# Halving the columns of some TensorE matmuls in a windowed-attention kernel, so that two steps are 1152 instructions

## The chip, the cores and the metric

The kernel runs on one core of a Trainium2 chip. The metric is the device time in microseconds (us) of one execution. The profiler's record of one execution stands beside it. TensorE is the matrix engine (PE in the profile, PEld its weight loads), DVE is VectorE, ACT is ScalarE, POOL is GpSimd, SP issues the transfers.

## The reference, cut to what matters

Input is `x` (16 sequences, 256 tokens, 128 channels), all fp32. A first part adds attention over windows of 64 tokens to it. The second part, on a layer norm of the result, runs six layers:

```python
for i in range(DEPTH):                                   # DEPTH = 6
    x = attn_layer(shift_tokens(x), Wqkv[i], q_scale[i], k_scale[i], Wo[i]) + x
    x = ffn_layer(shift_tokens(x), ln_g[i], ln_b[i], W1[i], b1[i], W2[i], b2[i]) + x

def attn_layer(x, Wqkv, qs, ksc, Wo):                    # 16 heads of 64, windows of 32
    q, k, v = heads(x @ Wqkv)                            # 128 -> 3 * 1024
    q, k = rotary(l2norm(q) * qs), rotary(l2norm(k) * ksc)
    sim = q @ k_of_own_and_previous_window * 8, masked
    return (softmax(sim) @ v).merge_heads() @ Wo         # 1024 -> 128
```

`ffn_layer` is a layer norm, a gated GELU layer of 2 x 341 columns and a product back to 128 channels.

## The kernel before, in words

The first part is a pipeline of its own over 32 tiles of 128 tokens (`first_stage`); it takes the first 280 us or so. The six layers then run as one pipeline whose unit is a block of 128 tokens: 32 blocks in a layer, 192 in all. The order of the work is written out by hand: each engine has a function (`step_pe`, `step_act`, `step_dve`, `step_pool`, `step_sp`) that is called for each step t = 0, 1, 2, ... and in it works on several blocks at once, block t in the projections, block t - 1 in the transposes and scores, block t - 3 in the weighted values and the output product. Everything is unrolled, so TensorE's program is one long stream of instructions without a branch in it. Engines meet by semaphores only.

Two steps make a pair, since a sequence has two blocks (`b = t % BLOCKS`, 0 or 1); in a step with b = 0 the feed-forward part does one share, in a step with b = 1 the other. On TensorE a step issues, in this order (before.py's lines 658 to 833):

1. `project` for q: six matmuls into one pair of banks. Each half of 512 columns (`UNIT`) has three, since a product of high and low parts takes the place of an fp32 one: high x high, low x high, high x low. The tokens (`xs_h`, `xs_l`) are the weights that are loaded, 128 x 128; 512 columns of `wq_h` or `wq_l` stream past. The type is F32R and such a matmul is one weight load and one matmul.
2. Eight transposes of the probabilities (`small,Sx`).
3. `project` for k, six matmuls.
4. Eight transposes of q (`small,qk`).
5. The weighted values, below called **the PT burst** (`PT,VB` and `PT,VA`): 64 fp32 matmuls with 64 x 64 weights and 32 columns. An fp32 matmul that is no transpose is issued as two weight loads and two matmuls, so the burst is 256 instructions, all in a row.
6. `project` for v, then eight transposes of k.
7. The share of the feed-forward part: with b = 0 the first product (`f_h,w_h`, `f_h,w_l`, `f_l,w_h`: 18 F32R matmuls of 256 columns), with b = 1 the second (`X,w_sb`), and four transposes.
8. The scores (`X,qT`): 32 fp32 matmuls with weights of 64 columns and 64 columns streaming.
9. The output product (`X,wo_sb`): eight fp32 matmuls, `PC[:, 0:P] += wo_sb[:, a, :].T @ oT[:, a, :]`, 128 x 128 weights and 128 columns streaming: 16 weight loads and 16 matmuls in the profile.

Who waits for this work: ACT squares q and k as soon as they are there (`q_done`, `k_done`), copies v (`v_done`), and DVE adds the output product to x (`y_done`, in `update_x`). Semaphore waits that don't fit on a matmul are instructions of their own in the stream. A helper records every matmul, so all have line 226 in the profile, and transposes 229; they are told apart by their tiles.

Of the kernel before, what the change touches and what calls it, by code (L numbers as in the profile page):

```python
# [13 lines left out]
P = 128  # L14
SEQS, LEN, DM = 16, 256, 128
TOKENS = SEQS * LEN
BLOCKS = LEN // P
# [5 lines left out]
INNER = HEADS * DH  # L23
PAIRS = HEADS // 2
UNIT = 512
KEYS = 2 * WIN
RING = 4
NBLOCKS = SEQS * BLOCKS
# [39 lines left out]
def build(nc, x_in, w_first, wqkv, wo, qkscale, fw1, fw2, vectors, c_rot, c_small, out):  # L68
    ctx = ExitStack()
    with ctx:  # L70
# [3 lines left out]
        def sem(name):  # L74
# [18 lines left out]
        wo_sb = sb("wo_sb", [P, PAIRS, DM])  # L93
# [23 lines left out]
        oT = flat_x1[:, KT:KT + INNER].rearrange("p (a q) -> p a q", a=PAIRS)  # L117
# [17 lines left out]
        PA0, PA1, PB, PC = (ctx.enter_context(nc.psum_tensor(f"pair{i}", [P, 1024], F32)) for i in range(4))  # L135
# [23 lines left out]
        S = {n: sem(n) for n in (*STEP, *PER_SEQ, *LOADS, *PARTS, *ONCE, *FIRST, "xf0", "xf1", "vb0", "vb1", "vb2", "vb3", "phase",   # L159
                                 "stored", "opened", "o_t", "o_sum", "zeroed",  # L160
                                 "cleared", "waited")}

        def apart(e):


            e.sem_inc(S["waited"], 1)
# [58 lines left out]
        def mm(out, lhsT, rhs, start=True, stop=True, **k):  # L225
            return T_.matmul(out, lhsT, rhs, start=start, stop=stop, **k)  # L226
# [385 lines left out]
        def blocks(pl, name, back, k):  # L612

            per = STEP[name]
            return pl.times(NBLOCKS * per) + ((pl.t - back) * per + k)
# [22 lines left out]
                for t in range(DRAIN, DRAIN + NBLOCKS):  # L638
                    step(e, pl.at(t))

        def project(layer, pair, high, low, first):
            w_high, w_low = wq_high[layer % 2], wq_low[layer % 2]
            for u in range(2):
                cols = slice(first + u * UNIT, first + (u + 1) * UNIT)
                out = pair[:, u * UNIT:(u + 1) * UNIT]
                mm(out, high, w_high[:, cols], True, False)
                mm(out, low, w_high[:, cols], False, False)
                last = mm(out, high, w_low[:, cols], False, True)
            return last

        def projections(t):
# [9 lines left out]
        def step_pe(e, pl):  # L661
            t, b, then = pl.t, pl.t % BLOCKS, (pl.t - 1) % 2
            one, other = projections(t)
            bank0, bank1, bank2 = feed_banks(t)
            fresh = t % NBLOCKS == 0
            layer = pl.turn + t // NBLOCKS
            if pl.has(0):
                if b == 0:
                    e.wait_ge(S["xs_ready"], seqs(pl, "xs_ready", t // BLOCKS, 2))
                s = (t // BLOCKS) % 2  # L670
                high, low = (x[:, s, b * P:(b + 1) * P] for x in (xs_h, xs_l))
                if pl.has(1):
                    e.wait_ge(S["rotated"], blocks(pl, "rotated", 1, 2))
                if pl.seq(11) is not None:
                    e.wait_ge(S["gated"], seqs(pl, "gated", pl.seq(11), 2))
                if pl.seq(12) is not None:
                    e.wait_ge(S["x_done"], seqs(pl, "x_done", SEQS + pl.seq(12), 1))
                if pl.seq(10) is not None:
                    e.wait_ge(S["x_kept"], seqs(pl, "x_kept", pl.seq(10), 1))
                if pl.last and pl.seq(14) is not None:  # L680
                    e.wait_ge(S["o_sum"], pl.seq(14) + 1)
                if fresh:
                    e.wait_ge(S["wq_low_q"], layers(pl, 2, t // NBLOCKS, 2))
                project(layer, one, high, low, 0).then_inc(S["q_done"], 1)
            if pl.has(3):
                e.wait_ge(S["weighed"], blocks(pl, "weighed", 3, 1))
                if pl.has(4):
# [5 lines left out]
                for a in range(PAIRS):  # L693
                    last = tr(PC[:, a * P:(a + 1) * P], Sx[:, then, a, :, :].rearrange("p w k -> p (w k)"))
                last.then_inc(S["pT_done"], 1)
            if pl.has(0):
                if pl.has(1):
                    e.wait_ge(S["v_kept"], blocks(pl, "v_kept", 1, 1))
                if fresh:
                    e.wait_ge(S["wq_low_k"], layers(pl, 2, t // NBLOCKS, 2))  # L700
                project(layer, other, high, low, INNER).then_inc(S["k_done"], 1)
            if pl.has(1):
                e.wait_ge(S["scaled"], blocks(pl, "scaled", 1, 1))
                if pl.has(3):
# [23 lines left out]
            if pl.has(0):  # L728
                e.wait_ge(S["rotated"], blocks(pl, "rotated", 0, 1))
                if fresh:  # L730
                    e.wait_ge(S["wq_low_v"], layers(pl, 2, t // NBLOCKS, 2))
                project(layer, one, high, low, 2 * INNER).then_inc(S["v_done"], 1)
            if pl.has(1):
                e.wait_ge(S["scaled"], blocks(pl, "scaled", 1, 2))
                e.wait_ge(S["qkT_kept"], blocks(pl, "qkT_kept", 1, 1))
# [49 lines left out]
            q = pl.seq(9)  # L785
            if q is not None:
                e.wait_ge(S["xn_done"], seqs(pl, "xn_done", q, 1))
                if pl.has(0):
                    e.wait_ge(S["rotated"], blocks(pl, "rotated", 0, 2))
                elif q:  # L790
                    e.wait_ge(S["x_kept"], seqs(pl, "x_kept", q - 1, 1))
                for h in range(BLOCKS):
                    last = tr(bank1[:, h * P:(h + 1) * P], f_xn[:, h, :])
                last.then_inc(S["turned_back"], 1)
# [27 lines left out]
                last.then_inc(S["s_done"], 1)  # L822
            if pl.has(3):
                e.wait_ge(S["o_kept"], blocks(pl, "o_kept", 3, 1))
                if pl.has(1):
                    e.wait_ge(S["qkT_kept"], blocks(pl, "qkT_kept", 1, 2))
                else:
                    e.wait_ge(S["pT_kept"], blocks(pl, "pT_kept", 3, 1))
                if (t - 3) % NBLOCKS == 0:
                    e.wait_ge(S["wo_loaded"], layers(pl, 16, (t - 3) // NBLOCKS, 16))  # L830
                for a in range(PAIRS):
                    last = mm(PC[:, 0:P], wo_sb[:, a, :], oT[:, a, :], a == 0, a == PAIRS - 1)
                last.then_inc(S["y_done"], 1)

        def step_act(e, pl):
# [397 lines left out]
        @block.sync  # L1233
        def _(sp):
            tiles_in = x_in.rearrange("(t p) d -> p t d", p=P)
            sp.dma_start(X1[:, 0:8, :], tiles_in[:, 0:8, :]).then_inc(S["x_in0"], 16)
            sp.dma_start(w1_raw[:, 0:w_first.shape[1]], w_first).then_inc(S["w_loaded"], 16)
            sp.dma_start(small[:, :], c_small).then_inc(S["c_loaded"], 16)
            sp.dma_start(X1[:, 8:16, :], tiles_in[:, 8:16, :]).then_inc(S["x_in1"], 16)
            sp.dma_start(X1[:, 16:24, :], tiles_in[:, 16:24, :]).then_inc(S["x_in2"], 16)  # L1240
            sp.dma_start(X1[:, 24:32, :], tiles_in[:, 24:32, :]).then_inc(S["x_in3"], 16)
            sp.dma_start(rot[:, :, :, :].rearrange("p a b c -> p (a b c)"), c_rot).then_inc(S["rot_loaded"], 16)
            sp.dma_start(wq_raw[:, :], wqkv[0, :, 0:INNER]).then_inc(S["wq_loaded"], 16)
            sp.dma_start(qks[:, :, :].rearrange("p a b -> p (a b)"), qkscale[0, :, :]).then_inc(S["qks_loaded"], 16)
            sp.dma_start(wo_sb[:, :, :].rearrange("p a b -> p (a b)"), wo[0, :, :]).then_inc(S["wo_loaded"], 16)
            sp.dma_start(w2_sb[:, :, :].rearrange("p a b -> p (a b)"), fw2[0, :, :]).then_inc(S["w2_loaded"], 16)
            sp.dma_start(vec_g[:, :], vectors[0, :, 0:2]).then_inc(S["g_loaded"], 16)
            sp.dma_start(vec_b1[:, :], vectors[0, :, 2:8]).then_inc(S["b1_loaded"], 16)
            sp.dma_start(vec_b2[:, :], vectors[0, :, 8:10]).then_inc(S["b2_loaded"], 16)
            for k in range(1, 3):  # L1250
                sp.wait_ge(S["wq_low_" + "qk"[k - 1]], 2)
                sp.dma_start(wq_raw[:, :], wqkv[0, :, k * INNER:(k + 1) * INNER]).then_inc(S["wq_loaded"], 16)
            for g in range(4):
                sp.wait_ge(S["a_resid"], nth("a_resid", 8 * g + 7))
                sp.dma_start(x1_kept[:, g * 8 * DM:(g + 1) * 8 * DM], flat_x1[:, g * 8 * DM:(g + 1) * 8 * DM]).then_inc(S["x1_stored"], 16)
            sp.wait_ge(S["cleared"], 1)
            sp.dma_start(w1_raw[:, :], fw1[0, :, :]).then_inc(S["fw1_loaded"], 16)
            steps(sp, step_sp)
            o = out.rearrange("(t p) d -> p t d", p=P)
            for q in range(SEQS):  # L1260
                sp.wait_ge(S["o_sum"], q + 1)
                sp.dma_start(o[:, q * BLOCKS:(q + 1) * BLOCKS, :], out_rows(q)).then_inc(S["stored"], 16)
            sp.wait_ge(S["stored"], 16 * SEQS)
# [36 lines left out]

        @block.tensor
        def _(pe):
            pe.wait_ge(S["c_loaded"], 16)
            pe.wait_ge(S["w_centred"], 1)
            first_stage(pe, first_pe)
            meet(pe, 1)
            pe.wait_ge(S["cleared"], 1)
            steps(pe, step_pe)
# [41 lines left out]
```

## Time and profile before

| | |
|---|---|
| time, median of 3 runs | 3254.94 us (3250.23 to 3259.81) |
| the profiled execution | 3258.42 us, of which the span of its instructions is 3256.6 us |
| mean granted clock of TensorE | 0.988 of full speed |
| TensorE matmul | 3119.6 us busy, 96% of the span |
| TensorE weight loads | 2720.0 us, 84% |
| VectorE | 2771.0 us, 85% |
| ScalarE | 2547.2 us, 78% |
| GpSimd | 2646.1 us, 81% |

The span and the execution's own time differ by 1.8 us, which lie around the first and the last instruction. Matmuls are pipelined, each recorded length overlaps the next; the time between the starts of two says what one costs in a row.

### The profile page before, as it was taken

What the parts mean: (1) busy time and instruction counts of PE and PEld (TensorE: products, weight loads), DVE (VectorE), ACT (ScalarE), POOL (GpSimd) and SP (SyncE); (2) the same over time, 40 slices, a digit from 0 to 9 for tenths busy, and PEclk for the clock granted to TensorE, in tenths of its full rate; (3) what the DMA queues carried; (4) which work ended last, traced back from release to release, by engine and by line L of the source; (5) the groups of instructions that cost most, each with busy time, mean ns of one, the idle gap of its engine ahead of it and who ended that gap; (6) DMA issues with size and microseconds to landing.
All of it is one profiled execution on the core that took longest, in us unless ns stands there. A gap on an engine that the chain in (4) does not pass through costs nothing.

```text
span 3256.6 us, 123131 instructions
## 1 busy us (share of the span) xinstructions
PE 3119.6 (96%) x52802; PEld 2720.0 (84%) x52802; DVE 2771.0 (85%) x3721; ACT 2547.2 (78%) x3699; POOL 2646.1 (81%) x2641
## 2 busy tenths in 40 slices
PE   7978999999999999999999999999999999999997
PEld 4646888888888888888888888888888888888886
DVE  7968888888888888888888888888888888888884
ACT  5756778887878788788878787887878787877876
POOL 6658888887888888888888888888888888888873
PEclk9989999999999999999999999999999999999999
DMA  2001111111111111111111111111111111111111
GB/s 66 15 19 38 46 40 43 41 39 43 37 46 48 40 36 46 37 48 41 46 36 41 37 53 41 41 39 42 39 46 46 43 35 41 41 44 39 40 39 49
DMA packets 62044, 134.01 MB, mean 41 GB/s; under 512 B 11584, under 2 KB 35264, under 8 KB 61504
## 3 DMA queue, kind: packets, MB, share of 16 engines
q1 hardware_dynamic: 61504, 126.14, 13.4%
q8 instruction: 421, 6.90, 0.9%
q14 instruction: 119, 0.97, 0.1%
HBM read 21.27 MB, written 4.19 MB: 8 GB/s over the span
## 4 chain that ended last, share of the span: by engine, by line
PE 91%; issue 3%; ACT 2%; POOL 2%; DVE 1%; DMA 0%; POOLq 0%; DVEq 0%; SPq 0%; ACTq 0%
PE pair L226 73%; PE pair L229 17%; POOL sq L414 1%; ACT qT L865 0%; ACT PT L846 0%; ACT sq L843 0%; POOL wq_l L977 0%; ACT X L882 0%; ACT X L870 0%; DVE VB L336 0%; ACT sq L855 0%; DVE qk L332 0%; ACT VA L878 0%; ACT qk L441 0%; DVE ts L993 0%
## 5 line engine op out<-in xcount | busy, mean ns | idle before, releaser
L1123 POOL TENSOR_TENSOR qk<-qk,ts 128x1024 f32<-128x1024 f32 x384 | 910.8, 2384 | 80.4 <-DVE ts L993 71.7
L1104 POOL TENSOR_TENSOR qk<-qk,rn 128x1024 f32<-128x1024 f32 x384 | 724.1, 1907 | 15.1
L989 DVE TENSOR_TENSOR qk<-pair,tab 128x1024 f32<-128x1024 f32 x384 | 468.5, 1220 | 271.5 <-ACT sq L843 265.8
L843 ACT ACTIVATE sq<-pair 128x1024 f32<-128x1024 f32 x192 | 196.9, 1025 | 445.2 <-PE pair L226 445.2
L226 PE MATMUL pair<-wq_h,xs_h 128*128 128x512 f32 x1154 | 513.8, 445 | 14.2 <-POOL xs_l L957 7.9
L1138 POOL TENSOR_TENSOR Sx<-Sx,rden 128x1024 f32<-128x1024 f32 x192 | 365.3, 1902 | 170.9 <-DVE rden L1055 170.9
L993 DVE TENSOR_TENSOR ts<-pair,tab 128x1024 f32<-128x1024 f32 x384 | 466.5, 1215 | 0.0
L997 DVE TENSOR_REDUCE ss<-sq 128x16 f32<-128x1024 f32 x384 | 464.2, 1209 | 0.0
L226 PE MATMUL pair<-wq_h,xs_l 128*128 128x512 f32 x1152 | 463.4, 402 | 0.7 <-issue 0.6
L226 PE MATMUL pair<-wq_l,xs_h 128*128 128x512 f32 x1152 | 462.1, 401 | 0.5 <-issue 0.3
L229 PEld LDWEIGHTS pair<-small,qk 128*128 128x128 f32 x3072 | 351.0, 143 | 84.7 <-issue 51.4
L229 PE MATMUL pair<-small,qk 128*128 128x128 f32 x3072 | 410.3, 277 | 6.9 <-POOL qk L1104 5.1
L226 PE MATMUL pair<-X,qT 128*64 128x64 f32 x12288 | 400.5, 224 | 8.5 <-ACT X L882 5.3
L226 PEld LDWEIGHTS pair<-X,qT 128*64 128x64 f32 x12288 | 374.0, 138 | 41.2 <-issue 41.2
L226 PE MATMUL pair<-PT,VA 64*64 64x32 f32 x12288 | 379.5, 219 | 25.6 <-issue 25.6
L226 PE MATMUL pair<-PT,VB 64*64 64x32 f32 x12288 | 380.7, 221 | 18.5 <-issue 16.1
L865 ACT ACTIVATE qT<-pair 64x1024 f32<-64x1024 f32 x384 | 389.7, 1015 | 6.4 <-PE pair L229 4.1
L226 PE MATMUL pair<-X,wo_sb 128*128 128x128 f32 x3072 | 393.9, 282 | 0.0
L226 PEld LDWEIGHTS pair<-PT,VB 64*64 64x64 f32 x12288 | 330.2, 135 | 55.6 <-issue 55.6
L226 PEld LDWEIGHTS pair<-X,wo_sb 128*128 128x128 f32 x3072 | 357.4, 192 | 12.9
L226 PEld LDWEIGHTS pair<-PT,VA 64*64 64x64 f32 x12288 | 332.6, 135 | 23.8 <-issue 23.8
L1010 DVE COPY pair<-small 128x1024 f32<-128x1024 f32 x192 | 235.7, 1228 | 61.6 <-ACT X L870 58.8
(124 smaller groups left out, 6672.2 us busy)
## 6 DMA issues: line engine op xcount, KB each, us to landing
VB<-VA SPq DMA_DIRECT2D x192, 384.0 KB, 3.5
VB<-VA SPq DMA_DIRECT2D x96, 128.0 KB, 3.5
wq_raw<-wqkv SPq DMA_DIRECT2D x18, 512.0 KB, 5.6
xf<-xT SPq DMA_DIRECT2D x96, 64.0 KB, 1.9
xf<-xT SPq DMA_DIRECT2D x96, 63.8 KB, 2.0
wo_sb<-wo SPq DMA_DIRECT2D x6, 512.0 KB, 3.5
X<-x_in SPq DMA_DIRECT2D x4, 512.0 KB, 6.7
x_kept<-X SPq DMA_DIRECT2D x4, 512.0 KB, 2.7
```

Source lines behind the costliest of these rows:

```text
L226: return T_.matmul(out, lhsT, rhs, start=start, stop=stop, **k)
L229: return T_.transpose(out, in_, ident if idn is None else idn)
L414: last = G_.tensor_tensor(h3(kx1[:, i % 2, w * UNIT:(w + 1) * UNIT], W1N), rep(kT1[:, w * W1N:(w + 1) * W1N], HALF1, W1N), bc(own_head, HA ...
L843: A_.activation(sq[:, 0, :], one[:, :], ACT.Square).then_inc(S["squared"], 1)
L865: last = A_.activation(qT[rows, :, :, odd * WIN:(odd + 1) * WIN], PC[rows, :].rearrange("p (a w q) -> p a w q", a=PAIRS, w=4), ACT.Copy)
L989: V_.tensor_tensor(h3(qk[:, now, kind, :], DH), h3(source[:, :], DH), rep(factors[:, 2 * kind, b, :], HEADS, DH), ALU.mult)
L993: V_.tensor_tensor(ts[:, kind, :].rearrange("p (h a c) -> p h a c", **halves), swapped, sines, ALU.mult).then_inc(S["rotated"], 1)
L997: V_.tensor_reduce(ss[:, kind * HEADS:(kind + 1) * HEADS], h3(sq[:, kind, :], DH), axis=AX.X, op=ALU.add).then_inc(S["summed"], 1)
L1010: V_.tensor_copy(h3(PB[:, :], P), rep(mask[:, bb * P:(bb + 1) * P], PAIRS, P)).then_inc(S["masked"], 1)
L1104: G_.tensor_tensor(x, x, bc(rn[:, then, kind * HEADS:(kind + 1) * HEADS], HEADS, DH), ALU.mult).then_inc(S["scaled"], 1)
L1123: G_.tensor_tensor(qk[:, now, kind, :], qk[:, now, kind, :], ts[:, kind, :], ALU.add).then_inc(S["added"], 1)
L1138: G_.tensor_tensor(x, x, bc(rden[:, now, :], HEADS, KEYS), ALU.mult).then_inc(S["weighed"], 1)
```

## The change

Four things, all of them on TensorE.

- `project` gets a number `halved`, 0 to 6: the last `halved` of its six matmuls are made in two halves of 256 columns. Per step with b = 0 these are 0 for q, 0 for k, 6 for v; with b = 1 they are 6, 6 and 5. With a few exceptions at layer changes and in the last layer, a pair of steps has 23 halved projection matmuls, that is 46 more instructions.
- The output product of a step with b = 0 is made in two halves of 64 columns for all eight of its matmuls (`WO_HALVED = (8, 0)`): 32 more instructions. The weights of a matmul are loaded again for its second half.
- Two waits that repeat an earlier one of the same engine are left out.
- 37 semaphore increments (`apart`) stand at the beginning of TensorE's stream, ahead of its first wait.

```diff
+        AHEAD = 37
+        HALVED = {0: (0, 0, 6), 1: (6, 6, 5)}
+        def halved(pl, k):
+            t, n = pl.t, HALVED[pl.t % BLOCKS][k]
+            if k == 2 and t == NBLOCKS:
+                n -= 1
+            if k == 2 and pl.last and pl.seq(13) is not None:
+                n -= 2 + t // BLOCKS % 2
+            return n
+        WO_HALVED = (8, 0)
-        def project(layer, pair, high, low, first):
+        def project(layer, halved, pair, high, low, first):
             w_high, w_low = wq_high[layer % 2], wq_low[layer % 2]
+            n = 0
             for u in range(2):
-                cols = slice(first + u * UNIT, first + (u + 1) * UNIT)
-                out = pair[:, u * UNIT:(u + 1) * UNIT]
-                mm(out, high, w_high[:, cols], True, False)
-                mm(out, low, w_high[:, cols], False, False)
-                last = mm(out, high, w_low[:, cols], False, True)
+                for x, w in ((high, w_high), (low, w_high), (high, w_low)):
+                    width = UNIT // 2 if n >= 6 - halved else UNIT
+                    for at in range(0, UNIT, width):
+                        last = mm(pair[:, u * UNIT + at:u * UNIT + at + width], x,
+                                  w[:, first + u * UNIT + at:first + u * UNIT + at + width],
+                                  n % 3 == 0 and at == 0, n % 3 == 2, skip_group_check=True)
+                    n += 1
             return last
...
-                if pl.has(0):
+                if pl.has(0) and pl.seq(11) is None:
                     e.wait_ge(S["rotated"], blocks(pl, "rotated", 0, 2))
...
-                if pl.has(1):
-                    e.wait_ge(S["qkT_kept"], blocks(pl, "qkT_kept", 1, 2))
-                else:
+                if not pl.has(1):
                     e.wait_ge(S["pT_kept"], blocks(pl, "pT_kept", 3, 1))
...
                 for a in range(PAIRS):
-                    last = mm(PC[:, 0:P], wo_sb[:, a, :], oT[:, a, :], a == 0, a == PAIRS - 1)
+                    width = P // 2 if a >= PAIRS - WO_HALVED[b] else P
+                    for at in range(0, P, width):
+                        last = mm(PC[:, at:at + width], wo_sb[:, a, :], oT[:, a, at:at + width], a == 0 and at == 0, a == PAIRS - 1,
+                                  skip_group_check=True)
...
         def _(pe):
+            for _ in range(AHEAD):
+                apart(pe)
             pe.wait_ge(S["c_loaded"], 16)
```

What this does to TensorE's stream, at two places. The first is the end of a step with b = 0 and the q projection of the step after it, before:

```order
L226 MATMUL pair<-X,qT 64x64 [waits masked,qkT_kept]
L226 MATMUL pair<-X,qT 64x64 x31
L226 MATMUL pair<-X,wo_sb 128x128 [waits qkT_kept,o_kept]
L226 MATMUL pair<-X,wo_sb 128x128 x7
L226 MATMUL pair<-wq_h,xs_h 128x512 [waits gated,rotated]
L226 MATMUL pair<-wq_h,xs_l 128x512
```

and after the change (the sizes are those of the output; an fp32 row of x1 is two weight loads and two matmuls):

```order
L226 MATMUL pair<-X,qT 64x64 [waits masked,qkT_kept]
L226 MATMUL pair<-X,qT 64x64 x31
L226 MATMUL pair<-X,wo_sb 128x64 [waits o_kept]
L226 MATMUL pair<-X,wo_sb 128x64 x15
L226 MATMUL pair<-wq_h,xs_h 128x256 [waits gated,rotated]
L226 MATMUL pair<-wq_h,xs_h 128x256
L226 MATMUL pair<-wq_h,xs_l 128x256 x2
```

Eight output products have become sixteen of half the width, with no work moved past another. The second place is what follows the PT burst of a step with b = 1, the v projection. Before:

```order
L226 MATMUL pair<-PT,VA 64x32 x4
L226 MATMUL pair<-wq_h,xs_h 128x512 [waits rotated]
L226 MATMUL pair<-wq_h,xs_l 128x512
L226 MATMUL pair<-wq_l,xs_h 128x512
L226 MATMUL pair<-wq_h,xs_h 128x512
```

and after the change:

```order
L226 MATMUL pair<-PT,VA 64x32 x4
L226 MATMUL pair<-wq_h,xs_h 128x512 [waits rotated]
L226 MATMUL pair<-wq_h,xs_l 128x256 x2
L226 MATMUL pair<-wq_l,xs_h 128x256 x2
L226 MATMUL pair<-wq_h,xs_h 128x256 x2
```

Five of the six matmuls are halved there. The order of the work is the same on every engine; only TensorE's stream has more instructions (115,109 where there were 107,919, counted as weight loads, matmuls and instructions that only wait or count), and a pair of steps has 1152 of them where it had 1077.

## Rows read from the trace of the kernel before

**Rows 1.** The page: span, busy time of each engine, and the chain that ended last

```profile
span 3256.6 us, 123131 instructions
...
PE 3119.6 (96%) x52802; PEld 2720.0 (84%) x52802; DVE 2771.0 (85%) x3721; ACT 2547.2 (78%) x3699; POOL 2646.1 (81%) x2641
...
PE 91%; issue 3%; ACT 2%; POOL 2%; DVE 1%; DMA 0%; POOLq 0%; DVEq 0%; SPq 0%; ACTq 0%
```

**Rows 2.** Stretches: length, busy time of PE, PEld, DVE, ACT, POOL, granted clock, DMA share, GB/s

```profile
893.20:924.40 31.20, 30.31 (x532) 26.91 (x531) 26.94 (x35) 24.77 (x35) 25.44 (x24) 1.00 0.22 66
924.40:958.80 34.40, 32.08 (x533) 28.29 (x532) 27.35 (x35) 24.86 (x35) 26.30 (x26) 0.95 0.12 33
1018.90:1049.10 30.20, 30.20 (x532) 26.78 (x531) 26.74 (x35) 24.68 (x35) 26.27 (x26) 1.00 0.13 37
...
928.10:931.50 3.40, 3.40 (x10) 2.71 (x11) 2.30 (x3) 1.54 (x2) 2.69 (x2) 0.50 0.02 5
```

**Rows 3.** What the matmuls that read PT waited for (the tile's view)

```profile
  issue: 41.7, 41
```

**Rows 4.** TensorE's timeline: end of a stalled PT burst; start and follower of an undisturbed one

```profile
942.39 0.32 PE L226 MATMUL pair<-PT,VB 64*64 64x32 f32 x8
...
943.70 0.30 PE L226 MATMUL pair<-PT,VA 64*64 64x32 f32 x8
944.97 0.26 PE L226 MATMUL pair<-PT,VB 64*64 64x32 f32 x5 [0.97 <-issue]
...
1003.55 0.32 PE L226 MATMUL pair<-PT,VB 64*64 64x32 f32 x8
...
1005.55 0.50 PE L226 MATMUL pair<-wq_h,xs_h 128*128 128x512 f32 x1
```

**Rows 5.** DMA queues of the page: packets, MB, share

```profile
q8 instruction: 421, 6.90, 0.9%
```

**Rows 6.** TensorE's timeline: matmuls of 512 and of 256 columns in a row

```profile
940.22 0.40 PE L226 MATMUL pair<-wq_h,xs_l 128*128 128x512 f32 x1
...
941.15 0.40 PE L226 MATMUL pair<-wq_l,xs_h 128*128 128x512 f32 x1
...
948.06 0.28 PE L226 MATMUL pair<-f_h,w_l 128*128 128x256 f32 x1
...
948.89 0.29 PE L226 MATMUL pair<-f_l,w_h 128*128 128x256 f32 x1
```

**Rows 7.** TensorE's timeline: whole runs of scores, output product, first stage

```profile
1010.34 2.09 PE L226 MATMUL pair<-X,qT 128*64 128x64 f32 x64
...
1012.36 2.05 PE L226 MATMUL pair<-X,wo_sb 128*128 128x128 f32 x16
1014.16 0.48 PE L226 MATMUL pair<-wq_h,xs_h 128*128 128x512 f32 x1
...
101.19 1.11 PE L226 MATMUL pair<-VA,PT 128*64 128x18 f32 x32
```

**Rows 8.** TensorE's timeline: the first matmuls of those runs and of one with 85 weight columns

```profile
1010.34 0.28 PE L226 MATMUL pair<-X,qT 128*64 128x64 f32 x2
1012.36 0.38 PE L226 MATMUL pair<-X,wo_sb 128*128 128x128 f32 x1
1009.47 0.35 PE L226 MATMUL pair<-f_h,w_h 128*85 128x256 f32 x1
```

**Rows 9.** Groups by form: weight loads, then matmuls (busy us, mean ns)

```profile
L226 PEld LDWEIGHTS pair<-X,qT 128*64 128x64 f32 x12288 | 374.0, 138 | 41.2 <-issue 41.2
L226 PEld LDWEIGHTS pair<-X,wo_sb 128*128 128x128 f32 x3072 | 357.4, 192 | 12.9
...
L226 PE MATMUL pair<-X,qT 128*64 128x64 f32 x12288 | 400.5, 224 | 8.5 <-ACT X L882 5.3 <-DVE pair L1010 3.2
L226 PE MATMUL pair<-X,wo_sb 128*128 128x128 f32 x3072 | 393.9, 282 | 0.0
L226 PE MATMUL pair<-VA,PT 128*64 128x18 f32 x1024 | 36.4, 214 | 0.0
```

More of the change, by code:

```diff
@@ L683, in step_pe @@
                     e.wait_ge(S["wq_low_q"], layers(pl, 2, t // NBLOCKS, 2))
-                project(layer, one, high, low, 0).then_inc(S["q_done"], 1)
+                project(layer, halved(pl, 0), one, high, low, 0).then_inc(S["q_done"], 1)
             if pl.has(3):
@@ L700, in step_pe @@
                     e.wait_ge(S["wq_low_k"], layers(pl, 2, t // NBLOCKS, 2))
-                project(layer, other, high, low, INNER).then_inc(S["k_done"], 1)
+                project(layer, halved(pl, 1), other, high, low, INNER).then_inc(S["k_done"], 1)
             if pl.has(1):
@@ L731, in step_pe @@
                     e.wait_ge(S["wq_low_v"], layers(pl, 2, t // NBLOCKS, 2))
-                project(layer, one, high, low, 2 * INNER).then_inc(S["v_done"], 1)
+                project(layer, halved(pl, 2), one, high, low, 2 * INNER).then_inc(S["v_done"], 1)
             if pl.has(1):
@@ L787, in step_pe @@
                 e.wait_ge(S["xn_done"], seqs(pl, "xn_done", q, 1))
-                if pl.has(0):
+                if pl.has(0) and pl.seq(11) is None:
                     e.wait_ge(S["rotated"], blocks(pl, "rotated", 0, 2))
-                elif q:
+                if not pl.has(0) and q:
                     e.wait_ge(S["x_kept"], seqs(pl, "x_kept", q - 1, 1))
```

## The prediction

> **What bounds the kernel now.** I begin with the page. TensorE is busy 96% of the span, and the chain that ended last runs through it for 91%, with 3% of "issue", time in which the engine waited for nothing that the profile shows [rows 1]. No other engine is over 85%. So TensorE's own stream sets the time, and a microsecond added to it should lengthen the kernel by one, as long as no other engine is near.
>
> The table of stretches shows that none is. I cut the six layers at the starts of the PT bursts, so that each stretch is one pair of steps. An undisturbed pair lasts 30.2 us and TensorE is busy for all of it, while VectorE has 26.7 and GpSimd 26.3 [rows 2]. Of 95 pairs 69 are like this (30.1 on average). The other 26 are longer: 31.2 us in one, 34.4 in another [rows 2]. Added up, the 26 lie 69 us over 30.2 each. This is the part that the change can win.
>
> Where is it lost? The waits of the matmuls that read PT name "issue" 41 times, 41.7 us in total [rows 3]; no semaphore is involved. The timeline shows one: the burst starts at 942.39, runs to the twelfth group of eight matmuls at 943.70, and goes on only at 944.97 [rows 4]. An undisturbed burst takes 1005.55 - 1003.55 = 2.00 us with its lead-out [rows 4]. Each of the 41 costs 1.28 us on average inside the burst, 52 us in sum. In 12 of them the clock granted to TensorE is at 0.50 (1.2 instead of 2.4 GHz) for 3.4 us behind the stall [rows 2]. That explains the rest: 34.4 is 30.2 and two stalls of 1.28 and another 1.6 us; 12 x 1.4 gives the missing 17.
>
> What the 41 have in common shows when the stream is counted. One queue moved 421 packets, 6.90 MB [rows 5], 16.4 KB each; weight loads and matmuls are 2 x 52802 [rows 1], with 2315 instructions that wait or count 107,919, and that is 256 to a packet. So this queue brings TensorE's instructions in blocks of 256. Each of the 41 stalls is at instruction 192 or 193 modulo 256 of the recorded stream, always the same place: a block's edge. In the example 12 x 8 = 96 matmuls with their 96 loads were made, and the 193rd instruction was late. A burst is 256 instructions, so each of the 192 has one edge in it. Where this lies at place 0 to 189 of the burst, none of 148 was stalled; from 192 to 254 all of 42 were but one; two at 255 were not. The burst is the densest part of the stream: 256 instructions in 2 us. With the edge in its last quarter the next block is asked for too late.
>
> **The change part by part.**
>
> *The edges.* Before, a pair of 1077 instructions moves the edge through the burst from pair to pair; so a quarter of the bursts is hit. With 1152, four and a half blocks, the edge alternates between two places 128 apart. I counted the new stream from its built order with the 37 increments ahead: the edge lies at 17 to 51 or 146 to 182, and at 83 to 110 in three bursts near the ends. None of these is in the last quarter; only the first two bursts of all have it there (250 and 244). So the stalls of the pairs go, and with them the spells of half clock: -69 us. The bounds are 0 (the place of the edge means something else) and -72 (against pairs of 30.1); if the edges are right but the half clock stays, -52.
>
> *Halved projections.* 23 in a pair. In a row, 512 columns cost (941.15 - 940.22) / 4 = 0.2325 us and 256 columns (948.89 - 948.06) / 7 = 0.1186 [rows 6]. Two halves are 0.237, so a halved matmul costs 5 ns more and a pair 0.11 us: 96 pairs, +10 us. Bounds: 0 (256 columns were at 0.116 at best) and +20.
>
> *Halved output products.* This is the term that decides. Today a step's 16 loads and 16 matmuls take 1014.16 - 1012.36 = 1.80 us [rows 7], 0.112 each. Halved, the columns that stream are the same in sum, but there are 32 loads of the full 128 weight columns. No row has 128 weight columns and 64 streaming ones in fp32, so I bound it.
>
> Low end: the scores have 64 and 64, and their 64 matmuls take (2.09 - 0.22) / 63 = 0.0295 each [rows 7, 9], two at a time in different halves of the array; that is 0.059 for two. If a load of 128 columns took no more, 32 x 0.058 = 1.86 us, +0.06 per step.
>
> High end: loads one behind the other. In the first stage 32 matmuls with 64 weight columns and only 18 streaming ones take (1.11 - 0.21) / 31 = 0.029 each [rows 7, 9], again 0.058 for two. In the scores it is 0.059 with 64 streaming columns, in the PT burst (943.70 - 942.39) / 11 = 0.119 for eight, so 0.059 for four, with 32 [rows 4]: whatever streams, 64 weight columns take 0.058 us. So the load binds there. How does it grow with its columns? The recorded lengths are 138 ns for 64 columns and 192 for 128 [rows 9], 54 more. And the first matmul of a run, whose load is not yet hidden, is longer than its followers by 0.05 us with 64 weight columns (0.28 against a group of 0.22), by 0.07 with 85 (0.35 against 0.28), by 0.10 with 128 (0.38 against 0.28) [rows 6, 8, 9]. Three values, all about 0.8 ns per column. So a load of 128 columns takes 0.058 + 0.054 = 0.112 us, just what an output matmul costs today: streaming hides the load now, with nothing to spare. Halved, the load binds: 32 x 0.112 = 3.58 us, +1.78 per step with b = 0. Such steps are 96: +171 us. I take this end, since three kinds of rows agree on it; for the low end speaks only that no row has the very form.
>
> The projections don't suffer in this way: their load of 0.112 fits under 0.118.
>
> The Trainium skill ("TensorE: Matmul & The Clock Gate", section "LDWEIGHTS (loading the stationary operand)") gives a weight load as its columns over 1.2 in ns, 107 ns for 128, whatever streams; an estimate from that alone is 32 x 0.107 = 3.42 us, +1.62 per step, and a total about 15 us below mine. Its section "Back-to-back issue gap" gives an isolated matmul of up to 64 columns some 60 cycles, with no load counted; that is the low end's case.
>
> *Waits left out and increments ahead.* The two waits repeat ones that an earlier instruction of the same engine has passed, so they free nothing: 0. The 37 increments run while TensorE waits for its first input: 0. Nothing is queued differently on other engines; the output product ends 1.8 us later, and DVE's addition to x waits for it, but the engines have 3.5 us per pair of slack.
>
> **Sum.** Against the profiled execution: 3258.4 - 69 + 10 + 171 = 3370 us. The median of the runs is 3.5 below that execution, so I forecast 3367, 3.4% slower. A pair becomes 30.2 + 0.1 + 1.8 = 32.1 us.
>
> **The rivals.**
>
> A, faster: the load hides after all. A step's output product takes 1.86 us, +0.06 x 96 = +6, and the sum is 3258.4 - 69 + 10 + 6 = 3205, or 3202 as a median. It decides where a half takes 0.075 us: 69 - 10 = 59 us over 96 steps are 0.61, on top of 1.80, over 32 halves. Below that the change wins. For it: the form was never seen, and the second half loads the same weights. Against it: the three readings above. Chance 0.10.
>
> B, slower still: the stalls don't go, because the place of the edge only went with something else, or because the count in front of the stream is off and the edges fall in the last quarter. With as many stalls as now: 3258.4 + 10 + 171 = 3439. Against it: 41 of 41 stalls are at one place modulo 256. Chance 0.04. The Trainium skill ("Runtime: NRT & Kernel Launch", section "Instruction fetch mechanics") also has blocks of 256 instructions, and says that crossing into one is mostly hidden; by that nothing could be won, and this would be the sum. The trace agrees on the size and not on the hiding, at 1.28 us a stall.
>
> C, no change: a load between both ends, near 0.075 us per half. Nothing points there; 0.02.
>
> **How the numbers follow.** The forecast has 0.84. Its own bounds: gain 52 to 72, projections 0 to 20, output product 159 to 174 (a load of 0.108, twice the 54 ns, to 0.113), so 3342 to 3397 as a median. The rivals left out are 0.16 already, so this part must be nearly whole; I give 3325 to 3405, some 10 us wider on either side. Faster by over 0.3% (about what a measurement can tell here): 0.10; within: 0.02; slower: 0.88.
>
> **What the profile after would show.** Right: "issue" before matmuls that read PT down from 41 to about two; the granted clock near 1.0 in the layers; output products with 64 columns spaced 0.112 us, their mean length still near 0.22; weight loads busy well above 84%; undisturbed pairs of 32.1 us. Wrong: output products of 64 columns spaced 0.06 (rival A), or 40 or more stalls inside the bursts (rival B), or pairs in which TensorE waits for DVE or GpSimd.

## The result, and the profile after

The changed kernel takes 3371.93 us, median of 4 runs (3371.81 to 3375.46), where the kernel before took 3254.76 us, median of 4 (3250.23 to 3259.81). The ratio is 1.0354, with a 95% interval of 1.0329 to 1.0380. It is slower by 3.5%. The forecast was 3367 us.

The page of the kernel after, span, instructions, busy time, the queue that brings TensorE's instructions, and the chain that ended last:

```profile
span 3370.1 us, 130321 instructions
...
PE 3280.0 (97%) x56516; PEld 3016.6 (90%) x56516; DVE 2776.3 (82%) x3721; ACT 2543.8 (75%) x3699; POOL 2648.8 (79%) x2641
...
q8 instruction: 449, 7.36, 0.9%
...
PE 93%; issue 2%; POOL 2%; ACT 1%; DVE 1%; DMA 0%; POOLq 0%; DVEq 0%; SPq 0%; ACTq 0%
```

Beside [rows 1], TensorE's two streams have grown by 160 and by 297 us, and no other engine by more than 6. The weight loads are now at 90%. "issue" in the chain has gone from 3% to 2%.

The matmuls that read PT, what they waited for (the tile's view, TensorE alone):

```profile
  issue: 0.7, 1
```

It was 41 times [rows 3]. The one that is left is in the second burst of the layers, with the edge at place 244; the first, with the edge at 250, goes through. Stretches of the kernel after, each one pair of steps from PT burst to PT burst, and the whole of the layers (columns as in rows 2):

```profile
917.50:949.60 32.10, 32.10 (x572) 30.07 (x571) 26.95 (x35) 24.72 (x35) 25.43 (x23) 1.00 0.22 64
...
260.40:3318.80 3058.40, 3041.02 (x54018) 2849.45 (x54016) 2560.10 (x3231) 2350.69 (x3233) 2475.76 (x2251) 1.00 0.14 40
```

Where pairs lasted from 30.2 to 34.4 us [rows 2], they now all last 31.8 to 32.3, save the first three and the last, which are shorter. The granted clock is 1.00 through the layers; the spells of 0.50 have gone with the stalls. TensorE is busy without a gap in both kinds of pair, so what a pair has gained must lie in the spacing of its matmuls. The timeline of the step with b = 0, and of the one behind it, shows which:

```profile
1963.12 2.09 PE L226 MATMUL pair<-X,qT 128*64 128x64 f32 x64
1965.13 3.79 PE L226 MATMUL pair<-X,wo_sb 128*128 128x64 f32 x32
1968.72 0.49 PE L226 MATMUL pair<-wq_h,xs_h 128*128 128x256 f32 x2
...
1981.78 2.05 PE L226 MATMUL pair<-X,wo_sb 128*128 128x128 f32 x16
1983.59 0.48 PE L226 MATMUL pair<-wq_h,xs_h 128*128 128x512 f32 x1
```

The halved product takes 1968.72 - 1965.13 = 3.59 us, 0.112 for each of its 32 matmuls. The whole one takes 1983.59 - 1981.78 = 1.81, 0.113 for each of 16. Half the columns stream in the same time. The groups by form say why busy time alone would not have shown it:

```profile
L226 PEld LDWEIGHTS pair<-X,wo_sb 128*128 128x128 f32 x4608 | 528.9, 192 | 12.9
...
L226 PE MATMUL pair<-X,wo_sb 128*128 128x64 f32 x3072 | 363.3, 276 | 0.0
```

A halved matmul is recorded with 276 ns, a whole one had 282 [rows 9]. Half the columns take 6 ns off a record of 282, and in a row each costs 112: the recorded length doesn't say what a matmul costs, the spacing does.

### Where the 113.5 us went

From the start of the first PT burst of the layers to that of the last but one are 95 pairs. They took 3210.8 - 280.2 = 2930.6 us before and 3315.7 - 280.1 = 3035.6 after, +105.0. The price per pair shows where no stall disturbs it. Such a pair lasts 32.03 us after (median). Here is one of the kernel before, and one of the run below in which the output product is left whole:

```profile
1295.04:1325.20 30.16, 30.16 (x529) 26.78 (x528) 26.75 (x35) 24.65 (x35) 25.39 (x24) 1.00 0.13 38
...
1801.34:1831.58 30.24, 30.24 (x553) 28.24 (x552) 26.78 (x35) 24.64 (x35) 25.41 (x24) 1.00 0.13 37
```

So the halved projections cost 0.08 per pair, and the product the other 1.78 or 1.79; 95 of each are +8 and +169. The rest of the +105.0, -72, is what the stalls had cost. Ahead of the first burst nothing changed (280.2 and 280.1). The other 8.6 us lie behind, where the pipeline runs empty. Its two last stretches, before:

```profile
3210.80:3219.50 8.70, 7.05 (x168) 6.45 (x168) 3.81 (x11) 5.08 (x10) 3.58 (x6) 1.00 0.06 18
3219.50:3256.60 37.10, 23.44 (x258) 20.27 (x258) 10.91 (x28) 23.00 (x39) 5.99 (x18) 0.95 0.23 65
```

and after:

```profile
3315.70:3327.50 11.80, 10.19 (x164) 9.08 (x165) 3.84 (x11) 5.01 (x10) 3.58 (x6) 0.71 0.04 13
3327.50:3370.10 42.60, 29.60 (x274) 24.91 (x274) 10.91 (x28) 22.87 (x39) 5.99 (x18) 0.76 0.20 56
```

They are the same instructions but for the last halved product (+1.8). The granted clock was 0.71 and 0.76 where it had been 1.00 and 0.95: in this execution TensorE did more of its last work at 1.2 GHz, and the remaining 6.8 us go with that. Why the clock fell there was not tried.

### The profile page after: what moved, and what is told of

The parts are those of the page before. It is cut to its first block, busy times and chain, and to the rows that moved or that the text cites. A ratio compares the mean times of both kernels' runs of the same rounds, so it can differ in the third digit from the quotient of the medians.

```text
span 3370.1 us, 130321 instructions
## 1 busy us (share of the span) xinstructions
PE 3280.0 (97%) x56516; PEld 3016.6 (90%) x56516; DVE 2776.3 (82%) x3721; ACT 2543.8 (75%) x3699; POOL 2648.8 (79%) x2641
## 4 chain that ended last, share of the span: by engine, by line
PE 93%; issue 2%; POOL 2%; ACT 1%; DVE 1%; DMA 0%; POOLq 0%; DVEq 0%; SPq 0%; ACTq 0%
PE pair L226 77%; PE pair L229 17%; POOL sq L414 1%; POOL wq_l L999 0%; ACT X L904 0%; DVE VB L336 0%; DVE qk L332 0%; ACT VA L900 0%; ACT PT L868 0%; ACT qk L441 0%; DVE ts L1015 0%; DMA w_raw<-w_first 0%; ACT qT L887 0%; POOL qk L395 0%; ACT sq L865 0%
## 5 line engine op out<-in xcount | busy, mean ns | idle before, releaser
L226 PE MATMUL pair<-X,wo_sb 128*128 128x64 f32 (+1 forms) x4608 | 560.2, 278 | 0.0
L226 PEld LDWEIGHTS pair<-X,wo_sb 128*128 128x128 f32 x4608 | 528.9, 192 | 12.9
L226 PE MATMUL pair<-wq_h,xs_h 128*128 128x256 f32 (+1 forms) x1816 | 512.6, 342 | 11.2 <-POOL xs_l L979 8.0
L226 PE MATMUL pair<-wq_l,xs_h 128*128 128x256 f32 (+1 forms) x1910 | 462.2, 306 | 0.1
L226 PE MATMUL pair<-wq_h,xs_l 128*128 128x256 f32 (+1 forms) x1910 | 460.8, 306 | 0.0
L229 PE MATMUL pair<-small,qk 128*128 128x128 f32 x3072 | 403.4, 274 | 6.4 <-POOL qk L1126 5.0
L226 PE MATMUL pair<-PT,VA 64*64 64x32 f32 x12288 | 372.5, 219 | 0.7 <-issue 0.7
L229 PEld LDWEIGHTS pair<-small,qk 128*128 128x128 f32 x3072 | 338.7, 141 | 32.1 <-issue 24.9
L226 PEld LDWEIGHTS pair<-wq_h,xs_l 128*128 128x128 f32 x1910 | 316.1, 189 | 14.1
```

The lines of the kernel that those rows point to most:

```text
L229: return T_.transpose(out, in_, ident if idn is None else idn)
```

## The experiments

Two theories had to be told apart in each half of the account. **The product**: does it cost 1.78 us more because the weights of 128 columns are loaded twice as often (the load binds), or because there are more instructions, or because a pair of steps now collides with something? **The edges**: are the stalls made by the place where a block of 256 instructions ends, as the prediction says, or did they go for another reason? Ratios are against the kernel before, on the same chip. The first three runs below belong to the first question, the others to the second.

### The output product left whole

```diff
-        WO_HALVED = (8, 0)
+        WO_HALVED = (0, 0)
```

> The changed kernel with the output product whole in all steps; a pair is 1120 instructions and the edge moves again, 49 bursts have it in the last quarter (13 pairs both, 23 one). Theory: the halved output product cost 171 us, the stalls come back with 13 x 3.4 + 23 x 1.7 = 83 us: 3370 - 171 + 83 = 3282 us. Rival A' (the halved output product is cheap, something else made the kernel slower): above 3400 us.

Measured: 3284.53 us (3273.74 to 3294.54), ratio 1.0081 (1.0052 to 1.0110). One of its undisturbed pairs:

```profile
654.20:684.30 30.10, 30.10 (x566) 28.20 (x559) 26.81 (x35) 25.55 (x36) 26.64 (x25) 1.00 0.13 38
```

With the halved projections alone an undisturbed pair takes 30.14 us on average, 0.08 more than before (30.06). So the 1.8 us are the product's. Most of what this kernel still loses to the one before is stalls: without the 32 instructions a pair is 1120 long, the edges wander again, and 48 bursts are stalled.

```profile
  issue: 52.0, 48
```

### The product halved in the kernel before

Only the output product of steps with b = 0 is halved in before.py, with nothing else.

```diff
-                    last = mm(PC[:, 0:P], wo_sb[:, a, :], oT[:, a, :], a == 0, a == PAIRS - 1)
+                    width = P // 2 if b == 0 else P
+                    for at in range(0, P, width):
+                        last = mm(PC[:, at:at + width], wo_sb[:, a, :], oT[:, a, at:at + width], a == 0 and at == 0, a == PAIRS - 1,
+                                  skip_group_check=True)
```

> The kernel before with one part of the change: the output product of steps with b = 0 in two halves of 64 streaming columns. A pair is 1109 instructions; 61 bursts have the edge in the last quarter, nearly all in pairs of two. Theory (the loads bind, 1.78 us per pair, and stalls stay): 3189 without stalls, +171, +25 double stalls of 2.9 = 3432 us, between 3405 and 3465, and the 32 matmuls take 3.6 us. Rival (the halved output product is slow only beside the halved projections): below 3300 us.

Measured: 3450.47 us (3443.74 to 3465.77), ratio 1.0597 (1.0565 to 1.0629).

```profile
743.40:775.30 31.90, 31.90 (x556) 28.50 (x549) 26.78 (x35) 24.61 (x35) 25.41 (x24) 1.00 0.13 35
```

The pair is back at 31.9 us, and 60 bursts are stalled. This one edit loses more than the whole change: it pays the product and keeps the stalls.

### The product halved by its weights

The same number of instructions, in the same places, but each half now has 64 of the weight columns and streams all 128 columns, so that a weight load is half as long.

```diff
-                    width = P // 2 if a >= PAIRS - WO_HALVED[b] else P
-                    for at in range(0, P, width):
-                        last = mm(PC[:, at:at + width], wo_sb[:, a, :], oT[:, a, at:at + width], a == 0 and at == 0, a == PAIRS - 1,
-                                  skip_group_check=True)
+                    if b == 0:
+                        for at in range(0, P, P // 2):
+                            last = mm(PC[at:at + P // 2, 0:P], wo_sb[:, a, at:at + P // 2], oT[:, a, :], a == 0, a == PAIRS - 1,
+                                      skip_group_check=True)
+                    else:
+                        last = mm(PC[:, 0:P], wo_sb[:, a, :], oT[:, a, :], a == 0, a == PAIRS - 1)
```

> The changed kernel, the same number of instructions at the same places, but the output product of steps with b = 0 is halved by its 128 weight columns (64 outputs each, all 128 columns streaming) instead of by its streaming columns. Theory (the time is that of a weight load, 0.112 us for 128 columns and 0.058 for 64, two in different halves of the array at a time): the 32 matmuls take 1.8 us again, -171 us, 3199 us, below the kernel before. Rival (twice the instructions cost twice the time, whatever their shape, or matmuls of 64 weight columns don't run beside each other when they stream 128): no gain, 3370 us.

Measured: 3282.54 us (3277.83 to 3283.64), ratio 1.0075 (1.0048 to 1.0103). The timeline, with the halved product and a PT burst behind it:

```profile
1764.94 1.92 PE L226 MATMUL pair<-X,wo_sb 128*64 128x128 f32 x32
1766.79 0.50 PE L226 MATMUL pair<-wq_h,xs_h 128*128 128x256 f32 x2
...
1771.61 0.32 PE L226 MATMUL pair<-PT,VB 64*64 64x32 f32 x8
...
1772.80 0.30 PE L226 MATMUL pair<-PT,VB 64*64 64x32 f32 x8
1774.18 0.26 PE L226 MATMUL pair<-PT,VA 64*64 64x32 f32 x4 [1.04 <-issue]
```

32 matmuls take 1766.79 - 1764.94 = 1.85 us, as against 3.59, with as many instructions. That settles the first question: it is the load of 128 weight columns that binds, at 0.112 us, and not the count of matmuls. What sets the 0.058 us of a matmul here is not settled: the scores, with 64 weight columns too but 64 streaming ones, cost 0.0295 each [rows 7], so the streaming columns may count here.

The forecast of 3199 us was still wrong, by 84. The lines below show what stepped in. The burst at 1771.61 has its edge at place 177, and is stalled. The kernel after has its edge at the same place of the same burst and goes through. 49 bursts are stalled here: the first two, and all 47 that follow them with an edge from 173 to 182. The instruction queue in a window of 0.4 us, cut in 40 slices of 0.01 us, shows the packet of such a block:

```profile
DMA  0000000000000009000000000000000000000000
...
q8 instruction: 1, 0.02, 16.5%
```

The window begins at 1771.60; behind 15 empty slices the packet starts, at 1771.75, when the burst has run for 0.14 us, and TensorE goes on 2.43 us after that. In the kernel after, the block of a burst that starts at 1749.49 (edge 177 as well, two pairs earlier) is fetched at 1746.35, 3.14 us ahead of it. The window there begins at 1746.20, and the packets behind the second gap are another queue's:

```profile
DMA  0000000000000009000000000000290744224909
...
q8 instruction: 1, 0.02, 22.2%
...
1749.49 0.32 PE L226 MATMUL pair<-PT,VB 64*64 64x32 f32 x8
```

So the place of the edge is only half of the condition. The other half is how early the packet starts. It is tempting to say that the slow product of the kernel after, which lies not far ahead of these bursts, gives the fetch 1.8 us. The run with the product left whole speaks against this: its product takes 1.8 us as well, twelve bursts of the same kind of step have the edge at 173 to 179, and none is stalled; their packets start 3.4 to 5.5 us ahead. What this kernel alone has is 64 instructions in 1.85 us in front of these bursts; the kernel after has 64 in 3.59, the run with the whole product 32 in 1.8. Whether that makes the packet late no run shows: I ran nothing that moves the packet alone.

### The edges put into the last quarter

In the kernel after only the number of increments is changed, so that each burst meets an edge 70 instructions earlier: places 17 to 51 become 203 to 237.

```diff
-        AHEAD = 37
+        AHEAD = 107
```

> The changed kernel with 107 increments at the head of TensorE's stream instead of 37, and nothing else. The instructions of the layers move by 70 places against the blocks of 256: in 92 of the 192 PT bursts the block's edge now lies in the last quarter (203 to 237), both bursts of every other pair. Theory (a late block stalls a burst whose last quarter holds the edge): 92 stalls instead of 2; before, pairs with both bursts stalled were 3.4 us longer on average, 46 such pairs are +156 us, so about 3526 us, between 3490 and 3560. Rival B (the edge's place is not the cause, or the length of 1152 by itself took the stalls away): 3370 us, as the changed kernel.

Measured: 3479.63 us (3476.63 to 3493.40), ratio 1.0692 (1.0649 to 1.0734). Three pairs in a row, with two stalls, with none, and with two and a spell of half clock:

```profile
646.90:681.20 34.30, 32.35 (x573) 30.24 (x575) 27.06 (x35) 24.74 (x35) 25.45 (x23) 1.00 0.12 33
681.20:713.20 32.00, 32.00 (x579) 30.11 (x583) 27.01 (x35) 25.67 (x36) 26.65 (x24) 1.00 0.12 35
713.20:749.30 36.10, 33.87 (x578) 31.76 (x574) 27.03 (x35) 24.82 (x35) 26.62 (x24) 0.95 0.11 31
```

A number in front of the program, with not one instruction of the layers touched, makes the kernel 108 us slower. The edges are the cause of the stalls. The size was 46 us below the expected one, and below its range of 3490 to 3560: of 92 bursts with the edge at 203 or later, 74 were stalled, by some 1.15 us each, and 18 were not. In those 18 the packet started 2.7 to 3.2 us before the burst, in the stalled ones from 0.15 before its start to 0.85 behind it: the same two kinds as above.

That the late packet is what TensorE waits for shows in all eleven traces together. Packets and instructions can be paired by counting both: one packet for each 256. Of some 4,800 blocks none is entered sooner than 2.15 us after its packet starts. At their usual pace the stalled bursts would have entered theirs 0.5 to 1.9 us after it; they entered it 2.2 to 3.0 us after.

And 70 more increments were not free, since the first matmul starts at 17.28 instead of 10.55:

```profile
17.28 0.45 PE L229 MATMUL pair<-small,VB 128*128 128x128 f32 x1 [17.28 <-issue]
```

### The increments alone

```diff
         def _(pe):
+            for _ in range(37):
+                apart(pe)
             pe.wait_ge(S["c_loaded"], 16)
```

This is before.py with nothing but the 37 increments.

> The kernel before with the 37 increments at the head of TensorE's stream and nothing else. The edge wanders through the bursts as before, 44 of them have it in the last quarter. Theory: no difference, 3250 to 3266 us. Rival (the increments themselves, by what they leave in front of the layers, take the stalls away): 3190 us.

Measured: 3254.39 us (3244.07 to 3266.71), ratio 0.9996 (0.9978 to 1.0014), with 41 stalled bursts. They cost nothing and, without a pair of 1152, win nothing: where the edges wander through all places, moving them all by 37 hits as many.

### Fillers instead of matmuls

The kernel after with the output product whole, and 32 semaphore increments behind it in steps with b = 0, to have 1152 instructions without the loads.

```diff
+                if b == 0:
+                    for _ in range(32):
+                        apart(e)
```

> The changed kernel with the output product whole and 32 semaphore increments behind it in steps with b = 0, so that every later instruction stands at the same place. Theory: an increment is done by the sequencer, ahead of the array, and 32 of them hide under the matmuls in the queue: 3370 - 171 = 3199 us. If each takes the sequencer 51 ns as its record says and none hides, +157 us: 3356 us. Either way no more than 2 stalls in the bursts.

Measured: 3636.36 us (3630.00 to 3642.00), ratio 1.1164 (1.1131 to 1.1197). Both expectations fell. The stalls in the PT bursts are gone (the view of the tile names two), so the count of 1152 does its work with any kind of instruction. But:

```profile
1794.46 2.05 PE L226 MATMUL pair<-X,wo_sb 128*128 128x128 f32 x16
1799.55 0.76 PE L226 MATMUL pair<-wq_h,xs_h 128*128 128x256 f32 x2 [3.04 <-issue]
1800.12 0.63 PE L226 MATMUL pair<-wq_h,xs_l 128*128 128x256 f32 x2
```

The next projection starts 5.09 us after the product's start, not 1.81: the increments lie 0.15 us apart in the record, 32 of them take 4.8 us, and they start only as the product does. Behind the gap a pair of halves is recorded with 0.63 us where 0.40 is usual: TensorE runs at half clock. A stretch of one pair shows it:

```profile
1773.00:1809.00 36.00, 32.96 (x561) 30.75 (x562) 27.42 (x35) 25.84 (x36) 25.47 (x24) 0.95 0.11 31
```

The gap is worth 3.3 us per pair, 5.09 - 1.81, and the half clock up to 2.5 more; nearly all pairs take 33.4 to 36.4 us.

### Halved by weights, and the edges moved

In the version halved by weights, more increments take all edges to earlier places.

```diff
-        AHEAD = 37
+        AHEAD = 52
```

> As the kernel whose output product is halved by its weight columns, with 52 increments at the head instead of 37; the edges then lie at 2 to 36 and 129 to 164 in the bursts instead of 17 to 51 and 146 to 182. There the 47 bursts with the edge at 176 to 182 were stalled though the changed kernel's were not. Theory (a block asked for too late; the danger begins nearer the middle of the burst than the kernel before showed, and depends on what comes just ahead): with all edges at 164 or before it no burst of the layers is stalled but the first two, a pair lasts 30.3 us, and the whole 3258 - 69 + 10 + 4 = 3203 us, 1.7% below the kernel before. Rival (halving by weight columns itself brings the stalls, wherever the edge is): 3280 us again.

Measured: 3229.41 us (3225.00 to 3237.11), ratio 0.9926 (0.9904 to 0.9947). This is faster than both kernels, by 0.7% against the one before. Four bursts are stalled. It is 26 above what I expected, and every second pair shows where. The pair from 925.30 to 956.40, beside the one before it:

```profile
895.10:925.30 30.20, 30.20 (x572) 28.09 (x571) 26.79 (x35) 24.66 (x35) 25.39 (x24) 1.00 0.24 68
925.30:956.40 31.10, 30.33 (x572) 28.13 (x571) 26.95 (x35) 24.79 (x35) 26.32 (x26) 1.00 0.13 37
```

and the v projection behind its second burst in the timeline:

```profile
942.09 0.50 PE L226 MATMUL pair<-wq_h,xs_h 128*128 128x256 f32 x2
942.43 0.40 PE L226 MATMUL pair<-wq_h,xs_l 128*128 128x256 f32 x2
943.60 0.50 PE L226 MATMUL pair<-wq_l,xs_h 128*128 128x256 f32 x2 [0.77 <-issue]
```

In these pairs the burst has an edge at place 2 to 8, and the next one follows 256 instructions later, just behind the burst, after little more than 2 us. That block is late too, by some 0.3 to 1.2 us. The kernel before had this as well: behind a burst with the edge at 0 or 1 its matmuls stood 1.0 and 1.1 us apart, with the edge at 4 still 0.5 and 0.65. It isn't the last quarter as such that is dangerous, it is a whole block run through in about 2 us.

### The same with 44 and 48 increments

Two more values of `AHEAD` in the same kernel, to weigh the loss behind the burst against the stalls in it.

> The kernel with the output products halved by their weights, with 44 increments ahead instead of 52. With 52 the edges lay at 158 to 164 of one burst in four (3 of 48 stalled), and at 2 to 8 of another; in that one the next edge, 256 instructions on, lay 2 to 8 instructions behind the burst, and the v projection there took 1.3 to 1.9 us from its first to its fourth matmul instead of 0.8, with the gap named issue. With 44 these places become 166 to 172 and 10 to 16. If the block that begins behind the burst is late because 256 instructions in 2 us leave too little time for it, eight instructions more, some 0.5 us, take most of this loss away: the pairs of 30.5 to 31.3 come down to 30.2 to 30.6, and 3229 becomes about 3208 (3200 to 3216). Rival: places from 166 on are already in the part where every such burst stalls, as with 37 increments at 176 to 182: then 24 or 48 stalls of 1.3 us and some half clock, and 3240 to 3280.

> The same with 48 increments ahead: edges at 162 to 168 and, behind the burst, at 6 to 12. By the theory of the late block half of the loss of the version with 52 goes (some 0.25 us in each second pair, 12 us): 3217 (3208 to 3228), and the bursts at 162 to 168 stall in a few cases at most. By the rival that a burst stalls from place 165 on, a part of them does: 3225 to 3260.

Measured: 3261.05 us (3249.73 to 3277.85), ratio 1.0015 (0.9997 to 1.0032) for 44, and 3252.53 us (3241.83 to 3258.01), ratio 0.9983 (0.9972 to 0.9995) for 48. The theory's half was right and not enough: with 44 the v projection behind the burst is back at its usual length in two of three pairs. In the timeline of its pair from 897.9, where the edge lies at 171 in the first burst, that burst is stalled (first row), and the v projection behind the second has no gap:

```profile
900.43 0.24 PE L226 MATMUL pair<-PT,VB 64*64 64x32 f32 x1 [1.07 <-issue]
...
916.06 0.50 PE L226 MATMUL pair<-wq_h,xs_h 128*128 128x256 f32 x2
916.40 0.40 PE L226 MATMUL pair<-wq_h,xs_l 128*128 128x256 f32 x2
916.64 0.40 PE L226 MATMUL pair<-wq_l,xs_h 128*128 128x256 f32 x2
```

The rival was right about the other burst. Each fourth burst, in all some 48, has its edge in the places of this table:

| increments | places of the edge | stalled in them | time, us |
|---|---|---|---|
| 52 | 158 to 167 | 3 | 3229 |
| 48 | 162 to 171 | 25 | 3253 |
| 44 | 166 to 175 | 40 | 3261 |
| 37 | 173 to 182 | 47 | 3283 |

Up to place 161 none of these bursts is stalled, from 173 on all are, and between them the same place can go either way: at 164, three of seven with 52 increments. There too the packet tells them apart. It starts 2.5 us or more ahead of the bursts that go through and from 0.15 before to 0.6 behind the start of the stalled ones. Both bursts of a pair, with edges half a block apart and a spread of some 35 places over the layers, hardly fit between "too late in this burst" and "too soon behind it". 52 was the best of the four tried.

## Why the prediction was right

**What bounds the kernel.** Right. TensorE's stream sets the time in both, and what was added to it came out one for one. No engine came near.

**Stalls gone, -69.** Right in size: no pair of the layers but the first has a stall, the half clock is gone, and the pairs are even. By the pairs above the gain was 72: two pairs that I had counted as undisturbed, of 31.2 and 31.5 us, had a gap just behind a burst with the edge at 255. Putting the edges back brought 74 stalls back. Two things in its reasoning were wrong. The count of bursts in the kernel before was wrong as I wrote it: 45 bursts had the edge at 192 to 254, and 41 of them were stalled; the four that were not had it at 192, 193, 197 and 198. None of the other 147 was stalled inside. And the border at 192 was that kernel's own. With the product halved by weights, stalls begin at 162. The prediction took the border as fixed; had it been 162 in the kernel after too, with its edges up to 182, a quarter of the bursts would have gone on stalling, as in rival B. That they didn't is luck: the prediction had no step for when the packet starts, and what spared these bursts is open.

**Halved projections, +10.** Nearly: +8, by the pairs of 30.14 us with the projections alone (and the two waits left out) against 30.06 before, 0.08 where 0.11 was forecast.

**Halved output products, +171.** Right: 3.59 us against a forecast 3.58, and +1.78 per step. The step that decided was to take the load of 128 columns as 0.058 + 0.054 from three kinds of rows [rows 6 to 9]. Halving by weights instead gave 1.85 us for the same count, the prediction's low end of 1.86. So both ends that I gave were true prices, of two different halvings. One sign was off: the mean recorded length of the halved matmuls is 276 ns, not near 220. The forecast didn't rest on it. The Trainium skill ("TensorE: Matmul & The Clock Gate", section "LDWEIGHTS (loading the stationary operand)") puts a load of 128 columns at 107 ns; this trace has 112 as a spacing, and the same section's point that the columns count is what these two kernels show.

**Waits left out, increments: 0.** Right for 37 increments, by the run with them alone; wrong as a rule, as 107 of them cost 6.7 us at the start. No run takes the two waits alone; they lie within the 0.08 us above.

**The sum.** 3370 against 3371.9 us for the profiled execution. Part of this is luck: the gain from the stalls was 3 us larger and the projections 2 us cheaper than forecast, and this stands against 6.8 us at the end, with a lower clock, that no step of mine foresaw.

**The rivals.** A needed a half below 0.075 us and got 0.112. B needed 40 stalls and got one; the Trainium skill ("Runtime: NRT & Kernel Launch", section "Instruction fetch mechanics"), which has the crossing mostly hidden, fits most of the 421 blocks here, and not the 41 that cost 1.28 us each.

## What to carry to other kernels

A matmul of few columns costs what its weight load costs, here 0.112 us for 128 weight columns in fp32; whoever must split one splits the side that is loaded, since half the streaming columns saved nothing and half the weight columns cost next to nothing (1.85 us against 1.81). Where an unrolled stream has stretches of 256 instructions in 2 us, look for gaps that only "issue" explains, and count whether they sit at one place modulo 256; if so, the length of the loop body and a few instructions in front of the program decide some per cent of the time. And price the padding before using it: the gain of some 70 us was real, and was paid with 171.

## What the hardware showed that I had not expected

- An instruction block is fetched mostly in two kinds: some 3 us or more ahead of the burst, or at about its start. (In the kernel after, five packets started only 1.0 to 1.2 us ahead of bursts with the edge at 175 to 179; these went through, entering the block 2.3 us or more after its packet.) In the second kind TensorE goes on about 2.4 us after the packet starts (1771.75 to 1774.18; in the version with 52 increments the block behind a burst had its packet at 941.16 and the matmuls at 943.60). What decides which kind it is stays open; the same place of the same burst had both in different pairs of the run with 107 increments.
- An increment of a semaphore on TensorE's queue takes 0.15 us, more than a weight load and a matmul of 256 columns together (0.119). Its record says 51 ns; only the distance between starts shows the cost.
- A gap of 1.3 us in a burst can be followed by 3.4 us at half clock, and does not always: behind 12 of 41 before, and in 15 of 37 pairs with stalls in the run with 107 increments. What makes the difference is not settled either.
